# Where a step's products of values stand among the scores, in a fused four-layer attention kernel

## The reference

```python
x = [8, 128, 32, 32]
# L0, non-local block: theta, phi, g are 1x1 convolutions; phi and g are max-pooled 2x2
f = einsum('bcn,bcm->bnm', theta_x, phi_x);  y = softmax(f) times g_x
x = bn(conv1x1(y, w_W)) + x
# L1, wavelet block: Haar split into four quarters, 1x1 fusion, 7x7 spatial gate,
#     channel gate, 1x1 projection, inverse Haar
x = reconstructed + x
# L2, attention with one head of 128 channels
h = group_norm(x, 16);  q, k, v = wq h + bq, wk h + bk, wv h + bv
x = x + conv1x1(softmax(q.k * C**-0.5) v, wp)
# L3, attention with 8 heads of 16 channels, then an MLP
xn = group_norm(x, 32);  q, k, v = split(w_qkv xn)
attn = softmax(einsum('bhdi,bhdj->bhij', q, k) * temp)
out = einsum('bhdj,bhij->bhdi', v, attn)
x = x + w_out out + b_out;  x = x + mlp(group_norm(x, 32))
```

## Time and profile before

| what | us |
|---|---|
| median of 3 runs | 1860.47 |
| lowest, highest | 1857.03, 1860.66 |
| the profiled execution, its own time | 1869.27 |
| its span, first to last instruction | 1867.8 |
| PE busy (matmuls) | 1565.2 |
| DVE busy | 1139.0 |
| ACT busy | 813.9 |
| POOL busy | 274.1 |
| mean granted TensorE clock | 0.87 of full |

### The profile page before, as it was taken

The page is one execution under the profiler, slowest core; times in us unless marked ns, Lnnn a source line. Parts: engine busy times, 40 slices in busy tenths (PEclk is TensorE's granted clock), DMA queues, the critical chain, the costliest instruction groups (busy, mean ns, idle before and its releaser), DMA issues.

```text
span 1867.8 us, 20837 instructions
## 1 busy us (share of the span) xinstructions
PE 1565.2 (84%) x6468; PEld 693.1 (37%) x6468; DVE 1139.0 (61%) x1912; ACT 813.9 (44%) x1514; POOL 274.1 (15%) x305
## 2 busy tenths in 40 slices
PE   6579679889889998799789898798888988986982
PEld 3236235433443335333353334333343335322430
DVE  5454674767567584776567574776657682756601
ACT  1113202465326552366326562365425562753770
POOL 5004102110220102101140101201030104010000
PEclk6789957998889799798899898898888899977995
DMA  2000112011110303003020303003030203022101
GB/s 50 12 12 6 15 25 52 6 33 37 30 37 3 80 1 61 9 14 67 14 52 7 74 7 54 18 1 80 5 60 6 46 23 64 7 68 42 26 16 35
DMA packets 31569, 58.64 MB, mean 31 GB/s; under 512 B 14678, under 2 KB 16862, under 8 KB 31456
## 3 DMA queue, kind: packets, MB, share of 16 engines
q1 hardware_dynamic: 27296, 50.41, 12.7%
q0 software_dynamic: 4160, 6.83, 2.4%
HBM read 14.37 MB, written 4.50 MB: 10 GB/s over the span
## 4 chain that ended last, share of the span: by engine, by line
PE 52%; issue 21%; DVE 8%; DMA 6%; SPq 5%; ACT 4%; POOL 4%; POOLq 0%; ACTq 0%; DVEq 0%
PE ps L1337 52%; SPq L689 3%; DVE x L1189 3%; DVE mx L1283 2%; DMA invw<-inverse_sums 2%; DMA qp<-q3h 2%; POOL acc L849 2%; ACT p L1015 2%; SPq L666 1%; SPq L692 1%; DMA inverse_sums<-inv 1%; POOL ogc L816 1%; ACT hn L928 0%; DVE x L1196 0%; DVE x L1195 0%
## 5 line engine op out<-in xcount | busy, mean ns | idle before, releaser
L1283 DVE TENSOR_REDUCE mx<-ps 128x1 f32<-128x512 f32 x1024 | 649.1, 683 | 254.5 <-PE ps L1337 252.6
L1015 ACT ACTIVATE p<-ps 128x512 f32<-128x512 f32 x1024 | 548.8, 600 | 299.1 <-PE ps L1337 297.1
L1337 PE MATMUL ps<-kp,qp 63*128 63x512 f32 x1024 | 418.2, 512 | 87.8 <-DVE mx L1283 42.9
L1337 PE MATMUL ps<-qp,kp 64*128 64x512 f32 x1024 | 387.7, 475 | 23.2 <-ACT p L1015 18.4
L1337 PE MATMUL ps<-p,vt 128*32 128x512 f32 x2048 | 289.2, 638 | 5.8 <-ACT p L1015 5.5
L1337 PEld LDWEIGHTS ps<-qp,kp 64*128 64x128 f32 x1024 | 169.1, 197 | 322.7 <-ACT p L1015 228.4
L1337 PEld LDWEIGHTS ps<-kp,qp 63*128 63x128 f32 x1024 | 176.0, 206 | 221.9 <-DVE mx L1283 136.1
L980 ACT ACTIVATE p<-ps 128x512 f32<-128x512 f32 x128 | 76.1, 597 | 224.9 <-PE ps L1337 188.2
L1337 PE MATMUL ps<-p,vT 128*128 128x512 f32 x256 | 143.7, 655 | 2.2 <-ACT p L980 2.0
L849 POOL TENSOR_TENSOR acc<-acc,p 128x512 f32<-128x512 f32 x96 | 126.0, 1312 | 69.8 <-ACT p L980 66.3
L1279 DVE TENSOR_REDUCE mx<-ps 128x1 f32<-128x512 f32 x128 | 84.3, 685 | 40.2 <-PE ps L1337 40.2
(11 more groups left out here) (192 smaller groups left out, 1666.6 us busy)
## 6 DMA issues: line engine op xcount, KB each, us to landing
qp<-q3h SPq DMA_DIRECT2D x128, 64.0 KB, 2.9
xin<-in_x SPq DMA_DIRECT2D x8, 512.0 KB, 4.5
acc<-inverse_sums SPq DMA_DIRECT2D x16, 256.0 KB, 3.4
kp<-k3h POOLq DMA_DIRECT2D x64, 64.0 KB, 4.1
qp<-q3l SPq DMA_DIRECT2D x64, 64.0 KB, 3.2
x3a<-x SPq DMA_DIRECT2D x8, 512.0 KB, 4.6
kp<-k3h SPq DMA_DIRECT2D x64, 64.0 KB, 2.5
x3b<-x3a SPq DMA_DIRECT2D x8, 512.0 KB, 2.9
```

The source lines that it names most:

```text
L1015: a.activation(p3[:, s % 2, i, :], ps[:, SB + (u + 1) % 3, :], ACT.Exp).then_inc(sem("p3_ready"), 1)
L1283: v.tensor_reduce(mx3[:, i, c, h:h + 1], ps[:, bank, :], AX.X, ALU.max).then_inc(sem("mx3_ready"), 1)
L1337: return nc.tensor.matmul(o, l, r, start=start, stop=stop)
```

## The change

The four products of a step's values move from lap i = 1 of the next step (behind that lap's score and its early maximum, ahead of its side work) to lap i = 2, ahead of that lap's score. Behind an early maximum and with nothing else in lap 1 both are the same place. They differ where lap 1 has side work or a late maximum: that now comes first. The copy of `og` on ACT goes from lap 2 to lap 3.

With it come new numbers in the tables:

- `STEADY`: on all engines the pieces of `queries` come one lap earlier (Q2: averages in lap 14 instead of 15, the products in 19, 22, 26, 30, 33, 37 instead of 20, 23, 27, 31, 34, 38); `projections` begins a lap earlier; `wavelet` begins in lap 0 instead of 1; the first two pieces of `non_local` in 105 and 108 instead of 107 and 110; `values2` of tiles 3 and 6 a lap earlier; some maxima sit in other laps.
- `FIRST`: other laps for the maxima of L2, the early part of the first image's `non_local`, and one matmul more that writes nothing used (`fill`, lap 49).
- `LAST`: other laps for `tail` and one filling matmul fewer (`beside`).

```diff
 STEADY = {
-    "values2": (1, 2, 3, 4, 5, 6, 7, 8, 11, 11, 12, 12, 13, 14, 15, 16),
+    "values2": (1, 2, 3, 3, 5, 6, 6, 8, 11, 11, 12, 12, 13, 14, 15, 16),
...
         "PE": {
-            "L1": {0: 1, 2: 2, 4: 4, 8: 8, 10: 8, 13: 10, 15: 11},
-            "Q2": {1: 15, 3: 15, 5: 20, 7: 23, 9: 27, 11: 31, 13: 34, 15: 38},
+            "L1": {0: 0, 2: 2, 4: 4, 8: 8, 10: 8, 13: 10, 15: 11},
+            "Q2": {1: 14, 3: 14, 5: 19, 7: 22, 9: 26, 11: 30, 13: 33, 15: 37},
...
         "Pool": {
-            "Q2": {4: 15},
+            "Q2": {4: 14},
...
@@ ACT
-                        if i == 2 and s and s % NC == 0:
+                        if i == 3 and s and s % NC == 0:
...
@@ PE, in passes, ahead of the scores of the lap
+                        if heads and 0 <= q < HEAD_LAPS and i == 2 and s:
+                            h, j = divmod(s - 1, NC)
+                            if j == 0:
+                                wait(pe, sem("og_ready"), bt, NG * NH, NH * g + h)
...
+                            wait(pe, sem("p3_ready"), bt, NG * TILES, g * TILES + GH * s)
+                            for k in range(GH):
+                                last = mm(ps[32 * k:32 * (k + 1), VB, :], vt3[g][:, j, k, :], p3[:, (s - 1) % 2, k, :],
+                                          start=j == 0, stop=j == NC - 1)
+                            last.then_inc(sem("pv3_done"), 1)
@@ behind the early maxima: the same lines, with i == 1, go
-                        if heads and 0 <= q < HEAD_LAPS and i == 1 and s:
...
```

More of the change, by code:

```diff
@@ L112 @@
             "Q3.0": {0: 0},
-            "L0.0": {0: 0, 18: 9},
+            "L0.0": {0: 0, 18: 12},
             "L0.1": {0: 18, 18: 35},
@@ L164 @@
             "L1": {0: 0},
-            "Q2": {4: 15},
+            "Q2": {4: 14},
             "Q3": {4: 47},
             "TL": {8: 89},
-            "L0": {26: 148},
+            "L0": {26: 152},
             "HN": {4: 8},
@@ L237 @@
             "Q3": {0: 0},
-            "TL": {15: 98},
-            "L0": {0: 98, 18: 132},
+            "TL": {15: 100},
+            "L0": {0: 100, 18: 132},
             "HN": {0: 3, 2: 3, 3: 4},
@@ L243 @@
     "fill": "000000000000000000000000000000000000000000000000000000000000000000000000000000000000000000000000000000000000000000000000000000000000000000000000000000000000000000000000000000000000",
-    "beside": 73,
+    "beside": 71,
 }
@@ L1623, in passes @@
                         s, i = divmod(q, GH)
+                        if heads and 0 <= q < HEAD_LAPS and i == 2 and s:
+                            h, j = divmod(s - 1, NC)
+                            if j == 0:
+                                wait(pe, sem("og_ready"), bt, NG * NH, NH * g + h)
+                                wait(pe, sem("vt3_ready"), bt, NG, g + 1)
+                                if g == 0 and h == 0:
+                                    wait(pe, sem("inv2_ready"), bt + 1, NH)
+                            wait(pe, sem("p3_ready"), bt, NG * TILES, g * TILES + GH * s)
[3 more added lines that the diff above has]
+                            last.then_inc(sem("pv3_done"), 1)
+                    for g in range(NG):
+                        q = p - HEADS_FROM[g]
+                        s, i = divmod(q, GH)
                         if heads and 0 <= q < HEAD_LAPS and s < STEPS:
@@ L1643, in passes @@
                         by_query(ring, entry)
-                    for g in range(NG):
-                        q = p - HEADS_FROM[g]
-                        s, i = divmod(q, GH)
-                        if heads and 0 <= q < HEAD_LAPS and i == 1 and s:
-                            h, j = divmod(s - 1, NC)
-                            if j == 0:
-                                wait(pe, sem("og_ready"), bt, NG * NH, NH * g + h)
-                                wait(pe, sem("vt3_ready"), bt, NG, g + 1)
-                                if g == 0 and h == 0:
-                                    wait(pe, sem("inv2_ready"), bt + 1, NH)
-                            wait(pe, sem("p3_ready"), bt, NG * TILES, g * TILES + GH * s)
-                            for k in range(GH):
-                                last = mm(ps[32 * k:32 * (k + 1), VB, :], vt3[g][:, j, k, :], p3[:, (s - 1) % 2, k, :],
-                                          start=j == 0, stop=j == NC - 1)
-                            last.then_inc(sem("pv3_done"), 1)
                     if attention:
```

6 lines of the change are left out of this document (3 added, 3 removed), and 30 rows, old and new, of tables (FIRST, LAST, STEADY).

## The result

| | before | after |
|---|---|---|
| runs, median us | 1860.57 (1857.03 to 1861.93, 4 runs) | 1838.04 (1830.19 to 1839.56, 4 runs) |
| ratio after / before | | 0.9869, 95% interval 0.9834 to 0.9904 |
| profiled span us | 1867.8 | 1838.0 |
| mean granted clock | 0.870 | 0.874 |

The medians stand 22.5 us apart, 1.2%. The prediction has 1851.4, 9.1 us under the run before: the direction is right, the size is not. The time lies at the very low end of the range that was given (1838), where rival 1, the clock, was put (1840).

What follows compares the result with a forecast made beforehand. PE, busy 84% of the span, was taken to set the pace nearly everywhere; 5 + 7 - 2.5 - 0.4 = 9.1 us off the median 1860.47 gave 1851.4, with an 8-in-10 range of 1838 to 1864.

Steps and rivals of the forecast that it cites:

- rival 1: Smaller waits spare the clock's second fall behind laps 14 to 17, windows 1 to 5: 11 us, 1840; chance 0.22.
- The move can't win by its own wait: Moved products of values wait only 5.8 us in 2048 instructions; gains must come from work let pass and the tables.
- Laps 14 to 17, 5 us: End of L2's attention, windows 0 to 5: earlier averages shorten waits up to the sums; 5 us, between 4.2 and 11.4.
- L1150 held by POOL: Laps 14 to 17: POOL's back-to-back sums may hold DVE's L1150 for 1.3 us more; held 4.2 us won, free 11.4.
- The heads' steps, 7 us: Heads' steps with a projection: three waits go, 1.4 us in each of six windows, 8.3; 7 taken.
- The first lap, 2.5 us of cost: `x,wfc` behind the first score waits about 0.6 us for DVE's `x1`: 0.5 lost in each of windows 1 to 5.
- Rival 3: Averages' new wait keeps the clock low through to the second fall, five windows: 14.4 us slower, 1865.8; chance 0.12.

Runs made afterwards that it cites:

- the move alone: Tables of before with only the code changed (products of values ahead of the next score, `og` copy to lap 3), against the kernel before: 1863.66 us, 0.9986.
- the averages alone: Kernel before with only the group norm's two averages and the DVE, ACT and POOL pieces beside them one lap earlier: 1845.26 us, 0.9875 of before.
- the steps alone: Kernel before with only the projections of Q2 and the first pieces and the last of Q3 one lap earlier: 1853.88 us, 0.9943 of before.
- the filling ahead of the sums: Kernel before with eight matmuls nobody reads put ahead of PE's wait for `ysb`, no table changed: 1850.25 us, 0.9897 of before.
- the changed kernel with the averages put back: Changed kernel with only the averages and the pieces beside them back in their laps of before: 1847.28 us, 0.9917 of before.
- the changed kernel's second: Profile of the unmodified changed kernel run again on another chip, against the kernel before there: 1834.39 us, 0.9836.
- the tables alone: Code of before with all table numbers of after, against the kernel before, run three times: 1830.22, 1832.45, 1832.92 us; 0.9795, 0.9813, 0.9828.
- the filling of lap 14: Kernel with tables of after and code of before, plus 14 unread matmuls in lap 14 ahead of the early maximum: 1833.69 us, 0.9834 of before.
- the late `ysb`: Tables of after, code of before, eight small ACT copies ahead of the `ysb` copy: 1846.23 us, 0.9860 of before; with eight unread matmuls added, 1833.86, 0.9822.
- the first comparison: First measurement of the changed kernel against the kernel before: 1838.04 against 1860.57 us, 0.9869.

## Why the prediction was wrong in size

The forecast was 9.1 us; the change gave 22.5 by the medians, and 30.6 us on another chip. The step that failed is the clock: the sum has no term for it. By its steps:

- **The move can't win by its own wait.** Right. The move alone gave 2.6 us, with an interval that takes in nothing, and the waits of its group fell by 2.0 in the changed kernel (5.8 to 3.8).
- **Laps 14 to 17, 5 us.** Right in size as far as can be told: up to the sums the six windows are 6.6 us shorter, 6.7 by the averages alone. But both are differences to one profile of before (335.5), and the move alone, the steps alone and the filling ahead of the sums, whose averages stand as before, take 331.5, 331.2 and 330.5, and the changed kernel with the averages put back 328.8. Seven profiles with the averages in lap 14 and nothing filled take 325.1 to 331.1. The means of the two sets, 331.5 and 327.9, leave 3.6 us. By windows the working is mixed. Window 0 loses 1.7 by the averages alone, as worked out (54.2 for 52.5). For windows 1, 2, 4 and 5 it had 1.4 each; they give 2.9, 2.7, 0.1 and 2.8. Window 1 does not read like window 2, as it says: its four adds took 1.43 us already before. The adds take 1.43 us in window 2, against the 1.7 that the prediction has. The average starts 0.05 us behind the statistics in windows 1 and 4, and 0.48 in windows 2 (744.54, less 743.86 plus 0.20) and 5, where 0.3 was given. The wait ahead of the sums is 0.75, under 1.
- **L1150 held by POOL.** Not seen. Its 24 instructions take 219 to 221 ns in the changed kernel:

```profile
L1150 DVE SCALAR_TENSOR_TENSOR mv<-mv,vec x24: 219/219/221, 99.0 to 1825.2; 128x1 f32<-128x1 f32 x24
```

  The prediction had POOL's two sums back to back; the second waits for its exponential and starts behind L1150. So the row says nothing on whether it would be held. The prediction calls the adds the nearest rows to L1150; a nearer one is L1148, directly ahead and as small (128x1), and it was held in both kernels.

```profile
L1148 DVE TENSOR_TENSOR mv<-mv,vec x24: 158/159/1231, 98.8 to 1825.0; 128x1 f32<-128x1 f32 x24
```

  In window 2 after it takes 1.23 us, from 747.07 to 748.30, and POOL's first sum goes from 747.02 to 748.28. The Trainium skill's GPSIMD Engine Reference, section Specifications, has GpSimd's SBUF interfaces contend with VectorE instructions that have two SBUF inputs; L1148 has two (`mv`, `vec`), and the trace agrees, as it does for the adds, which meet the sums less (1.43 for 2.38). For L1150 it could not be tested.
- **The heads' steps, 7 us.** Right in mechanism, and in size within the interval: 10.6 alone (6 to 15). The 0.68 us ahead of `wpv,hn` and the 0.36 are gone; the wait for `vT` was there before as well and remains. Timeline of PE, window 2 after, against the earlier trace rows:

```profile
766.20 1.12 PE L1337 MATMUL ps<-hn,wk_s 128*128 128x512 f32 x2
...
769.37 1.16 PE L1337 MATMUL ps<-wpv,hn 128*128 128x128 f32 x8
...
774.55 0.49 PE L1337 MATMUL ps<-qp,kp 64*128 64x512 f32 x1 [0.85 <-ACT vT L946]
```

- **The first lap, 2.5 us of cost.** The wait of 0.6 us is there against the earlier trace rows, but not in all five windows: in windows 1 and 2 of this profile (0.47 and 0.64 us), in windows 1, 2 and 5 of the changed kernel's second. That makes 1.1 to 1.7 us; whether it costs that is smaller than the runs can tell. Window 2:

```profile
699.76 2.00 PE L1337 MATMUL ps<-x,wfc 128*128 128x256 f32 x8 [0.64 <-DVE x L1196]
```

- **The clock.** This is the step that failed. The forecast's sum takes the granted clock as given, which puts its return at nothing; the return stands in rival 1, with a chance of 0.22 against 0.46, and with half of 22 us as its worth. The argument against it was that "new waits of the same total in smaller pieces stand earlier". The runs say otherwise: PE's idle time directly ahead of the sums decides most of it. With 2.5 us there the second fall came in all six windows, with 1.4 in five. With 0.75 or less, whether the wait had been made shorter or merely filled, it stayed away in most windows; in some the fall of lap 14 ran on through the sums, and in four (one of the changed kernel's second profile, three of the tables alone) the clock fell again for 3.4 us. The exception is the filling of lap 14, where the fall came late and lay behind the sums with a wait of 0.75. And the clock was under-priced: 16 to 19 us by the filling, where the prediction has 11; the late `ysb`, with and without PE filled, gives 7 to 12 for a part of it. Two things made it small. First, the fall behind the sums of window 0 (6.8 us, from 345.30) was not counted; with it the stretches are 51.2 us, not 44.3, and half of that is 25.6. Second, only half of the possible gain was taken, because PE would meet ACT and DVE; but the earlier trace rows show PE busy 10.20 of 10.20 us in the low stretch, with DVE at 4.65 and ACT at 3.94: nobody else is near being the bound there. The traces give 18.5 of the 25.6, seven tenths.
- **Rival 3, the slower side**, came in one window (5) in the first comparison, the one that won least. The Trainium skill's TensorE: Matmul & The Clock Gate, section A second HAM failure mode, tells of short idles between groups of matmuls that make the clock swing, at a cost. The trace agrees, and the late `ysb` gives a price here: 0.7 us more idle time a window, 6 to 13 us in the run. But the rule had been read for the wrong side. It spoke for the change, since the change takes idle time away at the point ahead of the stretch in which PE is the bound.

A slip of the sum changes nothing: the high ends add up to 11.4, 8.3 and -0.4, 19.3 us (1841.2), where 19 and 1841.6 are given.

With the measured parts the sum for the changed kernel is 3.6 to 6.7 (waits up to the sums), 10.6 (steps), 2.6 (the move) and 16 to 19 (clock), 33 to 39 us, for 30.6 measured; for the tables alone, without the move, 30 to 36, for 32 to 38. The steps' waits and the clock lie in the same stretch, from the sums to `og`, and overlap there: 12.1 and 18.5 us alone, 21.7 to 23.7 in the changed kernel's two profiles.

## What to carry to other kernels

When a stretch at the lower clock follows a wait of PE, and PE is busy all through that stretch, price the wait at its length plus up to half of the stretch (here seven tenths of the half came), not at its length; and before moving any work, fill that wait with matmuls that nobody reads, since this tells in one run what the clock is worth. The fall of laps 14 to 17, where PE waits for others, was worth nothing: filling there moved it in one kernel and removed half of it in the other, and neither got faster by it. And read the parts of a change apart from its title: here the numbers of the tables did all that can be seen, and the code that gave the change its name could have been left out.

## What the runs showed of the hardware

A difference of 0.7 us in one wait per window of about 210 us moved the median of a whole run by 13 us (6 by the ratios). Ten runs of that program on one chip spread over 35 us (1826.95 to 1861.55), along with a mean granted clock of 0.881 to 0.856. Twelve runs of the same kernel without the delay, on three chips, spread over 12 us (1824.05 to 1835.58), and twelve of the kernel before on one chip over 22 (1855.66 to 1877.28).

Filling a wait of 4.3 us did not remove the fall behind it: in window 2 the granted clock fell at 745.20 and again at 752.00, where the tables alone fell at 740.9, and the waits that were left behind the filling are 0.98, 0.62, 1.12 and 0.75 us.

A DVE instruction on 128x1 elements, 0.16 us by itself (median of L1148), took 1.23 us when it started 0.05 us behind a POOL sum of 128x512 that took 1.26: it ended with that sum.
